# One core: routing in two halves, an earlier tanh, a held GpSimd product, and TensorE products that nobody reads

## The reference

```python
# 1: a recurrence over the 64 positions, for each of the 32 rows
logits = concat([x, h]) @ W_attn.T + b_attn;  aw = softmax(logits)
comb = relu(concat([x, aw @ enc]) @ W_comb.T + b_comb)
h    = tanh(comb @ W_ih.T + b_ih + h @ W_hh.T + b_hh);  out = h @ W_out.T + b_out
# 2: 64 experts and a shared one; each token goes to 8 experts out of 4 of 8 groups
scores = sigmoid(x @ router_w.T);  coef = 2.5 * scores[top 8] / sum, elsewhere 0
h   = silu(x @ Wg[e]) * (x @ Wu[e]) * coef[:, e];  moe = sum over e of h @ Wd[e]
# 3: self attention, cross attention, gated feed forward, each behind an adaptive norm
# 4: x @ weight.T + pooled(x) @ disha
```

## Time and profile before

| what | value |
|---|---|
| time, median of 3 runs | 1178.45 us (1174.59 to 1179.83) |
| the profiled execution's own time | 1180.14 us |
| its span, first to last instruction | 1178.4 us |
| mean granted TensorE clock | 0.868 |
| busy: PE, DVE, ACT, POOL | 1022.0, 719.5, 452.7, 526.2 us |

### The profile page before, as it was taken

The page is one execution under the profiler, slowest core; times in us unless marked ns, Lnnn a source line. Parts: engine busy times, 40 slices in busy tenths (PEclk is TensorE's granted clock), DMA queues, the critical chain, the costliest instruction groups (busy, mean ns, idle before and its releaser), DMA issues. The chain is left out here.

```text
span 1178.4 us, 29839 instructions
## 1 busy us (share of the span) xinstructions
PE 1022.0 (87%) x12382; PEld 683.7 (58%) x12382; DVE 719.5 (61%) x1719; ACT 452.7 (38%) x829; POOL 526.2 (45%) x464
## 2 busy tenths in 40 slices
PE   3798987799989999899978995899999899997967
PEld 3577875555545555455533443677777677775545
DVE  5535435455476546854576664777877777875453
ACT  2322213122222213122222222687787677785111
POOL 4688401033422324223354563676676576664010
PEclk9555555589889999898999997999999999999879
DMA  9020026122122222212223440000000000000000
GB/s 250 20 59 1 1 47 125 41 70 58 55 55 59 73 55 71 56 50 64 72 72 94 118 114 1 2 3 3 3 3 2 3 3 3 3 3 3 1 18 18
DMA packets 46057, 51.56 MB, mean 44 GB/s; under 512 B 22086, under 2 KB 36584, under 8 KB 45928
## 3 DMA queue, kind: packets, MB, share of 16 engines
q1 hardware_dynamic: 43010, 48.71, 15.8%
q10 hardware_dynamic: 2918, 1.01, 0.5%
HBM read 48.13 MB, written 1.57 MB: 42 GB/s over the span
## 5 line engine op out<-in xcount | busy, mean ns | idle before, releaser
L658 POOL TENSOR_TENSOR ex<-ex,xn 128x512 f32<-128x512 f32 x128 | 163.3, 1276 | 329.2 <-DVE ex L1194 241.2
L833 ACT ACTIVATE thcb<-ps 128x512 f32<-128x512 f32 x132 | 78.9, 597 | 276.0 <-PE ps L1539 275.1
L730 POOL TENSOR_TENSOR wu<-encC,wu 128x1024 f16<-128x1024 f32 x64 | 137.1, 2156 | 57.7 <-ACT encC L900 57.7
L1189 DVE SCALAR_TENSOR_TENSOR ex<-thcb,ps 128x512 f32<-128x512 f32 x132 | 90.6, 686 | 113.9 <-ACT thcb L833 111.5
L1546 PE MATMUL ps<-ex,wd 128*128 128x512 f32 x256 | 142.5, 639 | 1.6 <-DVE xT L1200 1.1
L1539 PE MATMUL ps<-xnT,wg 128*128 128x512 f16 x384 | 113.9, 409 | 5.8 <-DVE ex L1194 5.8
L1539 PE MATMUL ps<-xnT,wu 128*128 128x512 f16 x384 | 113.6, 408 | 0.0
L1487 PEld LDWEIGHTS ps<-eb,encC 128*128 128x128 f16 x3072 | 86.9, 99 | 32.6 <-DVE eb L1055 18.6
L1594 PE MATMUL ps<-wg,M 128*128 128x128 f16 x1536 | 97.4, 221 | 2.1 <-DVE wg L1280 2.1
L724 POOL TENSOR_TENSOR wd<-wd,a_sum 128x512 f32<-128x512 f32 x64 | 66.6, 1042 | 68.6 <-DVE a_sum L1311 68.6
L1594 PEld LDWEIGHTS ps<-wg,M 128*128 128x128 f16 x1536 | 92.3, 99 | 6.8 <-DVE wg L1280 2.5
(11 more groups left out here) (302 smaller groups left out, 1830.2 us busy)
## 6 DMA issues: line engine op xcount, KB each, us to landing
xn<-coef_rows SPq DMA_DIRECT2D x128, 256.0 KB, 3.8
thcb<-in_L_ffn_Wg SPq DMA_DIRECT2D x8, 256.0 KB, 3.8
thcb<-in_L_ffn_Wu SPq DMA_DIRECT2D x8, 256.0 KB, 3.1
wd<-in_L_ffn_Wd SPq DMA_DIRECT2D x2, 1024.0 KB, 10.1
xtok<-in_x SPq DMA_DIRECT2D x4, 256.0 KB, 5.8
thcb<-in_ctx SPq DMA_DIRECT2D x2, 512.0 KB, 10.7
wu<-in_L_xcond_attn_wq SPq DMA_DIRECT2D x2, 512.0 KB, 10.8
wu<-in_L_xcond_attn_wk SPq DMA_DIRECT2D x2, 512.0 KB, 10.6
```

The lines of the kernel that those rows point to most:

```text
L658: nc.gpsimd.tensor_tensor(hid[:, side(m, n), :], gu[:, side(m, n), :], other, ALU.mult)\
L730: nc.gpsimd.tensor_tensor(z[:, 1, 8 * u:8 * u + 8, :], a_Zc[:, u], z[:, 0, 8 * u:8 * u + 8, :], ALU.subtract)\
L833: nc.scalar.activation(th[:, side(m, n), :], bank(side(m, n)), ACT.Tanh, scale=0.5 / WSCALE)\
L1189: V.scalar_tensor_tensor(ga[:, :], th[:, side(m, n), :], 1.0, bank(side(m, n)), add, mul)\
```

## The change

The names of the parts are those of the diff.

1. **Routing in halves.** Chunk 0 is routed as before, in steps 16 to 23. Chunks 1 to 3 are each routed in two halves of two tiles: the first in the second half of the chunk's own steps (from gap 64m + 32), the second in the first half of the next 16 steps. A table `HALF` gives their gaps (0 to 27). The projection's bias becomes one product over all tiles in place of one for each tile. `coefT` uses transposes in place of f32 products and has a tile of its own. The "+ 1" of the sigmoid moves from DVE to ACT; two DVE operations of the mask become one.
2. **tanh behind the gate product.** The semaphore `gu_ps` is parted into `g_ps` (after the three gate matmuls) and `u_ps` (after the three of up). ACT waits for the first, DVE waits for the second ahead of gu.
3. **GpSimd pinned.** In steps with units GpSimd waits, ahead of hid, for the tanh of the next unit (place 1) or for `diag` of the next step (place 3).
4. **Products without a reader.** In all gaps below 96 TensorE does 1 to 5 f16 products of 512 columns into bank 5, which nothing reads.
5. **Order of the setup groups.** The group of the norm weights and those of the wv transposes stand ahead of a product group, not behind it.

```diff
+        WHOLE = {0: ("project",), 2: ("residual",), 4: ("x1T",), 6: ("stats",), 10: ("xn2T",), 12: ("router",), 14: ("sig0", "sig1"),
+                 15: ("sig2", "sig3"), 16: ("sfc",), 18: ("top1",), 19: ("top2",), 20: ("more",), 22: ("equal", "rank"), 23: ("mask",),
+                 26: ("pick", "take0", "take1", "take2", "take3"), 27: ("sum",), 28: ("inverse",), 30: ("coef",), 31: ("coefT",)}
+        HALF = {0: ("project",), 2: ("residual", "stats"), 4: ("x1T",), 8: ("xn2T",), 10: ("router",), 12: ("sig0",),
+                14: ("sig1", "sfc"), 16: ("top1",), 18: ("top2", "more", "equal"), 20: ("rank",), 22: ("mask", "pick"),
+                24: ("take0", "take1"), 26: ("sum", "inverse", "coef"), 27: ("coefT",)}
+        PARTS = [(0, 0, TPC, GAPS, WHOLE)]
+        for m in range(1, CH):
+            PARTS += [(m, 0, TPC // 2, GAPS * m + GAPS // 2, HALF), (m, TPC // 2, TPC, GAPS * (m + 1), HALF)]
...
                 if at in PASS_AT:
-                    unit(*PASS_AT[at])
+                    m, n = PASS_AT[at]
+                    t = k * SPC + st
+                    if place == 1 and t < T and (m, n) != chunk_units[-1]:
+                        pool.wait_ge(s["th_ready"], m * UNITS + n + 2)
+                    elif place == 3 and t + 1 < T:
+                        pool.wait_ge(s["diag_ready"], t + 2)
+                    unit(m, n)
...
-                act.wait_ge(s["gu_ps"], done + 1)
+                act.wait_ge(s["g_ps"], done + 1)
...
+                dve.wait_ge(s["u_ps"], done + 1)
                 V.tensor_tensor(gu[:, side(m, n), :], ga[:, :], bank(2 + side(m, n)), mul).then_inc(s["gu_ready"], 1)
...
-                    for t in range(TPC):
+                    mm(bank(7)[:, cols(ts)].rearrange("p (t d) -> p t d", d=P), ones_row[:, :],
+                       bout_row[:, :].unsqueeze(1).broadcast_to([1, len(ts), P]), start=True, stop=False, skip_group_check=True)
+                    for t in ts:
                         hs = Hc[:, t * TL:(t + 1) * TL, :].rearrange("p t b -> p (t b)")
-                        mm(bank(7)[:, t * P:(t + 1) * P], hs, w_outT, start=True, stop=False)
-                        last = mm(bank(7)[:, t * P:(t + 1) * P], ones_row[:, :], bout_row[:, :], start=False, stop=True)
+                        last = mm(bank(7)[:, t * P:(t + 1) * P], hs, w_outT, start=False, stop=True, skip_group_check=True)
...
+            def fill(count):
+                for _ in range(count):
+                    mm(bank(5), encC[:, 0, 0, :], encC[:, 0, 0:4, :].rearrange("p j d -> p (j d)"), start=True, stop=True)
+
+            for at, k, st, place in schedule():
                 if k < CH:
                     rnn(k, st, place)
+                if at < GAPS + U0:
+                    fill(1 if place in (1, 2) or at in LATE else 5 if place == 0 else 3)
```

More of the change, by code:

```diff
@@ L380, in build @@
                 n_folded = len(groups)
+            groups.append(product)
         for a in range(2):
@@ L489, in schedule @@
                 k, gap = divmod(at, GAPS)
-                yield at, k, gap // IDLE_GAPS, gap % IDLE_GAPS, PRO.get(gap) if 1 <= k <= CH else None
+                yield at, k, gap // IDLE_GAPS, gap % IDLE_GAPS
         block = ctx.enter_context(nc.Block())
@@ L559, in _ @@
             sp.wait_ge(s["setup_ps"], N_RNN)
-            coef_pass(0)
-            with sp.Fori(0, CH - 1) as j:
-                coef_pass(j + 1)
+            for m in range(CH):
+                coef_pass(m)
             outv = out.rearrange("b t d -> (b t) d").rearrange("(n p) d -> p n d", p=P)
@@ L818, in part @@
                 elif p == "coefT":
-                    act.wait_ge(s["coefT_ps"], m + 1)
-                    if not first(m):
+                    act.wait_ge(s["coefT_ps"], w + 1)
+                    if m:
                         act.wait_ge(s["coef_stored"], 16 * m)
[L822 to L826, removed]
+                    nc.scalar.copy(coefT[:, cols(ts)], bank(7)[0:E, cols(ts)]).then_inc(s["coefT_ready"], 1)
@@ L838, in _ @@
             all_evacuated(act, N_RNN - 1)
-            for at, k, st, place, p in schedule():
+            for at, k, st, place in schedule():
                 if k < CH and place == 0:
@@ L850, in _ @@
                     setup(g)
-                part(k - 1, p)
+                for what in PRO.get(at, ()):
+                    part(*what)
                 if at in UNIT_AT:
@@ L1105, in part @@
                         last = V.bn_aggr(mv[:, t, :], stats[:, t, :])
[L1106 to L1107 removed]
+                        if t < ts[-1]:
+                            mark(last)
                     last.then_inc(s["stats_ready"], 1)
[L1109 to L1131 removed]
@@ L1517, in part @@
                 elif p == "router":
[L1518 to L1519 removed]
+                    pe.wait_ge(s["xn2_next_ready"], w + 1)
+                    for t in ts:
                         last = mm(bank(7)[:, t * E:(t + 1) * E], xn2_next[:, t * P:(t + 1) * P], w_routerT,
@@ L1523, in part @@
                 elif p == "coefT":
-                    pe.wait_ge(s["coef_ready"], m + 1)
-                    for t in range(TPC):
-                        last = mm(bank(7)[0:E, t * P:(t + 1) * P], left[:, t, :], ident[:, :], start=True, stop=True)
+                    pe.wait_ge(s["coef_ready"], w + 1)
+                    for t in ts:
+                        last = nc.tensor.transpose(bank(7)[0:E, t * P:(t + 1) * P], left[:, t, :], ident[:, :])
                     last.then_inc(s["coefT_ps"], 1)
```

253 lines of the change are left out of this document (133 added, 120 removed).

## The result

The changed kernel takes **1137.53 us** in the median of 4 runs (1130.46 to 1143.40), beside 1177.25 us of the kernel before (4 runs, 1174.59 to 1179.83): a ratio of **0.966 [0.960, 0.972]**, faster. Its profiled execution took 1143.40 us, with a span of 1141.6, 5.9 us above its median. The forecast was 1128.0 within 1100 to 1168. So the time is inside the range and 9.5 us above the forecast; but two terms of the sum were far off, and they stood against each other, so that the closeness of the total is partly luck.

What follows compares the result with a forecast made beforehand. It took slow TensorE to bound steps 4 to 14, the recurrence's chain steps 15 to 23, and nearly TensorE the steps with units. Sum: 1180.1 - 16 - 13 - 10 - 13 = 1128 us, range 1100 to 1168.

Steps and rivals of the forecast that it cites:

- Routing in halves: Steps 24 to 63: five halves at 5.1 us each, 25.5 against 35.8 for two whole routings, -10 us.
- tanh behind the gate product: Steps with units: earlier tanh removes TensorE's idle time ahead of L1480, 30 steps x 0.44 us, -13 us.
- The fills: Steps 0 to 23: 152 products nobody reads raise TensorE's clock to 1.00 three quarters of the time, -16 us.
- What bounds the kernel: Slow TensorE in steps 4 to 14, the recurrence's chain in 15 to 23, nearly TensorE again with units.
- The worth of full clock: First 24 steps: 0.8 us a step on its own products, 19 us, plus 17 us on setup groups.
- fills as load: Rival, chance 0.12: the clock stays low and products nobody reads are load, +41 us on their term, 1185 us total.
- the 2.2: At half clock, unread products cost about 2.2 us in each of 9 later steps, 20 us.
- The pin: GpSimd's waits ahead of hid in steps with units: hid up to 1.3 us later, cost 0.
- The tail: Stretch behind the recurrence: 20.8 us too much, one half of routing left at 8 us, -13 us.
- DVE as the bound: Rival, chance 0.15: DVE's 76 short operations bound the steps with units, losing the 13 and 10, 1158 us.
- Full clock: Rival, chance 0.2: full TensorE clock throughout the first 24 steps, -35 in place of -16, 1109 us.
- What the text said would show it: Early clock 0.8 or more, steps 0 to 23 in 165 us, routing steps 8 to 8.5, last stretch 121.

Runs made afterwards that it cites:

- whole routing: The changed kernel with chunks 1 to 3 routed whole instead of in halves: 1151.41 us, ratio 0.9771 to the kernel before.
- the early tanh alone: The kernel before with only the unit's tanh moved behind the gate product: 1148.63 us, ratio 0.9781 to the kernel before.

## Why the prediction was right, and where it was not

By stretches of the profiled executions the forecast of -52 us met -36.8: -16 was +16.4 in steps 0 to 25, -23 was -41.4 in steps 26 to 63, -13 was -10.0 in the tail, and the rest, put at 0, was -1.8. The mechanisms of the tanh, of the pin and of the routing carried the gain; the fills had the wrong sign, and it was luck that steps 26 to 63 gave 18 us more than forecast and covered over half of the 32 that the fills' stretch was off.

**What bounds the kernel**: right for the steps with units. With the idle time gone TensorE is busy 57.59 of 57.59 us. For the first 24 steps the clock was named as the gate, and there the reasoning went astray.

**The fills: the step that failed.** It priced them at -16, "about three quarters of the time at 1.00". No run shows that share: over steps 0 to 23 of the changed kernel the mean clock is 0.63, about a quarter of the time at 1.00. Measured, steps 0 to 25 became 16.4 us longer in the profiled execution. Taking the fills out again gives 13.6 us by the spans (1141.6 to 1128.0) and 0.0075 or 9 us by the ratios; adding them to the kernel before costs 11.5 by the spans and 17.5 by the ratio. So they cost 9 to 17 us; the intervals of the whole change and of the kernel without fills touch (0.960 and 0.9616), but all three comparisons have the same sign. Without fills steps 0 to 25 take 197.4 us, 3.2 less than before, which is the 3 that the sum gave to the group order and the cheaper projection (neither was run alone). Three parts of the step fell. The clock: 0.50 in all of steps 4 to 14, where it mattered most. The rise was argued from the first unit, where 512-column products stood almost alone; with four such products in a step, among f32 products of 128 columns and 48 of two columns, the clock did not rise, and with ten its mean was 0.63. The worth of full clock: where it came (step 17) the step was 0.3 us shorter and not 0.6, since the 1.9 us from L1518 to L1522 are set by DVE and ACT at either clock (the weight load of L1522 waits 0.17 us for `diag` at 1.00, and L1480 0.16 at 0.50), and the fills at place 3 stand on the path (the next L1518 begins 0.25 us behind the end of the tanh, and 0.05 without fills). And the weighing: "fills as load" was given 0.12 with +41; the mechanism was that one, but smaller, because a fill in steps 4 to 14 cost 0.24 us and not 0.43, and of the 5.6 us of the nine steps behind them 5.1 fell on two, at the slow clock (3.0 and 2.0 us, near the 2.2 of the sum), while the sum had all nine pay. (The two terms that it names for the 2.2, 0.8 and 0.9, make 1.7.) Nor was it enough to have next to no idle time: in the 101.6 us of steps 4 to 14 TensorE had one, of 2.1 us, and the clock stayed at 0.50. Why the clock stayed low there stays open: TensorE was busy for 99.5 of the 101.6 us, and no run here parts the kinds of product.

**tanh behind the gate product**: the mechanism was right to the letter (the recurrence's tanh at the end of L1535, no idle ahead of L1522, a step without routing at TensorE's own length). The size was not: 13 for 27.7 alone and 21 undone. The mean of 0.44 us was already one over all steps, those without idle time too, and was then multiplied by 30; by 40 it is 17.8, and the profiles give (61.15 - 57.59)/8 = 0.445. Of the other 10 us some 6 are clock falls in steps 26 to 31 and 56 to 62 (a mean of 0.93 and 0.94 before, 1.00 with the early tanh), which the sum did not have: steps of 9.18 and 10.27 us stood there before where 7.52 and 8.60 are the rule, and with the early tanh they are 6.94 and 7.99. The other 4 lie in the two routings (78.46 us became 72.61, 78.54 became 72.93, at a clock of 0.89 before and 0.93 with it). That the falls come from the idle time is argued, not shown: they went when it went, but steps 40 to 47 of the kernel before have the same idle time (58.01 of 61.15 us busy) at a clock of 1.00.

**Routing in halves**: 5.1 for a half, measured 3.3 (5.0 with a fall); a whole routing 17.9, measured 17.3. Five halves are 16.5 (18.2 with the fall) in place of 25.5, so the term was -18 and not -10. Of a half, TensorE has 2.8 (60.35 less 57.59 us busy), near the 2.4; of the 1.5 of late DVE 0.5 came, and the 1.2 for a fall, which no row gave, came in one half of five, as 1.7. Taken from the same profiles the terms close: 38 x 0.445 = 16.9, 2 x 17.3 - 5 x 3.3 = 18.1, and some 7 of falls outside of routing (the excess of steps 26 to 31 and 56 to 62 over the regular steps) make 42, of 41.4 measured.

**The pin**: "cost 0" was right (61.16 for 61.15 us), but its gain stood hidden inside the routing term as one of several reasons. It is the edit on which the halves depend: undoing it costs 25.6 us in steps 26 to 63, and turns halves from a gain of 6.3 a chunk into a loss of 4.0.

**The tail**: -13, measured -10.0. But halving, which the term spoke of, gives only 1.6 of it; 133.3 to 124.9 comes with whole routing already, from the smaller edits (one bias product, `coefT` by transposes, fewer DVE operations) and the early tanh; that alone gives 0.8, and the pin does not act there. Which of the smaller edits gives the 7 us was not parted.

**The rivals.** DVE as the bound did not come: it is busy 41.1 of 60.9 us, and TensorE 60.4. Full clock did not come either. What the text said would show it: the clock (0.8 or more) wrong (0.63), steps 0 to 23 in 165 us wrong (192.4), the units' steps (57.59 us for eight) and the tanh right, routing operations below 1 us right in steps 26 to 63 and wrong in the tail (L1191, 1.28), routing steps of 8 to 8.5 us too long (7.03 to 8.10, one of 8.97), tail 121 near (123.3).

## What to carry to other kernels

On an engine that was 92% busy a product that nobody reads cost 0.24 us, of the 0.40 for which it holds the engine, and the clock it is meant to buy has to be shown on exactly that mix of products first; here neither of the two counts tried paid. When two edits work on the same queue (halving the routing, keeping GpSimd out of its way), price them in pairs: halves lost 4.0 us a chunk without the pin and won 6.3 with it. And a mean of idle time over all steps is to be multiplied by all steps; falls of the clock that go with it can add as much again in some stretches (6.1 us for 2.4 of idle time in steps 26 to 31, where the clock went from 0.93 to 1.00).

## What was not expected of the hardware

- TensorE busy 99.5 of 101.6 us, with four fills in each step of steps 4 to 14, kept a granted clock of 0.50; busy 112.5 of 112.8 us with ten of them it had 0.63. Steps with units, each with twelve 512-column f16 products and the f32 down products, have 0.99 over steps 26 to 63.
- Before, with TensorE idle for 0.5 us in three steps of four, the clock fell to 0.50 in some steps with units (0.93 over steps 26 to 63) and in others not (1.00 over steps 40 to 47); without the idle times it is 0.97 with the early tanh alone and 0.99 in the changed kernel.
- Without the pin four DVE operations of a half, with two inputs in SBUF, begin while GpSimd's hid runs and end 0.05 to 0.15 us behind it (0.29 us became 1.21 for L1195); ga and gu, with an input in PSUM, keep their 0.69 us beside it. In steps 26 to 63 of the changed kernel without the pin DVE is busy 21.0 us longer, 17.0 of them in such operations, and the steps take 25.6 us longer.
